# Gather stage: place and counting one-hots compared with numbers in PSUM, bucket numbers as int16, ten short lookups added

## The reference

```python
h1 = relu(einsum('ni,rij->nrj', x, weight1) + bias1)      # 8 relations
h2 = einsum('nrj,rjo->nro', h1, weight2)
msg = h2[src, edge_type] * edge_weight1                   # one row for each edge
agg = segment_sum(msg, dst)                               # layer 1 = relu(agg + bias2)
# layer 2: softmax of edge_weight1 over the edges of one dst, weighted sum of x[src]
# layer 3: two rounds of normalised neighbour sums (dinv[src] * dinv[dst])
# layer 4: gate = silu(attr @ W1.T + b1) @ W2.T + b2 + sum(emb[z[src]] * (emb[z[dst]] @ adaptW.T))
#          msg = gate * x[dst] * (cos cutoff * mult[dst]), summed by src, divided by sum of mult[dst]
```

## Time and profile before

| what | value |
|---|---|
| time, median of 3 runs | 6396.96 us (6395.7 to 6403.15) |
| profiled execution: span, first to last instruction | 5440.4 us |
| what lies around the span | not given by the page; the median is 956.6 us above the span |
| POOL busy | 3976.1 us (73%) |
| DVE busy | 4017.9 us (74%) |
| PE busy, weight loads | 3563.1 us (65%), 2831.5 us (52%) |
| gathers of the stage (L1046) | 1616, 168.0 to 2273.6 us |

### The profile page before, as it was taken

How to read it: one execution, slowest core, us unless ns; L and a number is a source line. 1 busy time by engine, 2 the same in 40 slices (tenths; PEclk the granted TensorE clock), 3 DMA queues, 4 the chain that set the end, 5 groups by cost and what they waited for, 6 DMA issues and landing times.

```text
span 5440.4 us, 122612 instructions
## 1 busy us (share of the span) xinstructions
PE 3563.1 (65%) x46841; PEld 2831.5 (52%) x46841; DVE 4017.9 (74%) x7211; ACT 2632.6 (48%) x5527; POOL 3976.1 (73%) x4023
## 2 busy tenths in 40 slices
PE   8355555555555555347766777777777768988885
PEld 7355555433333333225555555555555568977774
DVE  5555555666666666627888888888888888789999
ACT  2111111111111111226667667677676767888885
POOL 3677777777777777677777777777777764349996
PEclk7555555555555555556666665666676679999998
DMA  5566522222222222124444444444444446877774
GB/s 169 186 211 195 163 60 59 58 68 58 60 59 58 60 59 58 39 40 77 81 75 78 81 76 80 82 80 78 80 79 76 82 90 188 229 200 216 212 213 128
DMA packets 1135509, 576.38 MB, mean 106 GB/s; under 512 B 752611, under 2 KB 1074543, under 8 KB 1134785
## 3 DMA queue, kind: packets, MB, share of 16 engines
q1 hardware_dynamic: 1030017, 457.40, 35.3%
q0 software_dynamic: 104896, 110.96, 9.0%
HBM read 399.84 MB, written 168.16 MB: 104 GB/s over the span
## 4 chain that ended last, share of the span: by engine, by line
POOL 47%; issue 15%; PE 12%; DVE 12%; SPq 6%; DMA 4%; ACT 4%; POOLq 0%; DVEq 0%; ACTq 0%
POOL ring L1046 29%; POOL by_src L1058 9%; PE ps L1612 4%; DMA meta_a<-in_attrT 2%; SPq L866 2%; POOL meta_b L1184 2%; POOL meta_b L1181 2%; PE ps L1436 2%; DVE dst_i L2803 2%; DVE meta_b L2793 2%; DVE big L2824 2%; PE ps L1426 2%; SPq L863 1%; PE ps L1220 1%; POOL ring L1184 1%
## 5 line engine op out<-in xcount | busy, mean ns | idle before, releaser
L1058 POOL DMA_INDIRECT by_src<-meta_a,row_src x1612 | 1624.9, 1008 | 517.1 <-issue 474.3
L1046 POOL DMA_INDIRECT ring<-h_table,meta_b x1616 | 1614.9, 999 | 508.2 <-issue 490.6
L1679 ACT ACTIVATE ring<-ring,meta_b 128x48 f32<-128x48 f32 x1616 | 386.1, 321 | 1727.8 <-DMA ring<-h_table,meta_b 1727.8
L1388 PE MATMUL ps<-ring,WX 128*128 128x48 bf16 x2188 | 417.5, 237 | 894.0 <-DVE row_src L2430 894.0
L1388 PEld LDWEIGHTS ps<-ring,WX 128*128 128x128 bf16 x2188 | 367.0, 168 | 915.1 <-DVE row_src L2430 915.1
L2793 DVE TENSOR_TENSOR meta_b<-big,ps 128x1152 bf16<-128x1152 bf16 (+1 forms) x546 | 698.8, 1280 | 0.0
L1426 PE MATMUL ps<-meta_a,w1T 40*48 40x256 f32 x806 | 381.0, 568 | 465.0 <-DMA meta_a<-in_attrT 282.0
L1518 PE MATMUL ps<-WX,meta_b 128*128 128x49 bf16 (+1 forms) x14742 | 557.3, 197 | 35.7 <-ACT meta_b L1774 16.4
L1518 PEld LDWEIGHTS ps<-WX,meta_b 128*128 128x128 fp8e4 (+1 forms) x14742 | 543.1, 105 | 42.0 <-issue 24.6
L2429 DVE TENSOR_TENSOR row_src<-ring 128x384 f32<-128x384 f32 x202 | 112.7, 558 | 582.6 <-ACT ring L1679 582.4
L1436 PEld LDWEIGHTS ps<-w2T,meta_a 113*128 113x128 f32 x1612 | 325.1, 283 | 338.1 <-issue 297.3
(11 more groups left out here) (388 smaller groups left out, 8954.2 us busy)
## 6 DMA issues: line engine op xcount, KB each, us to landing
by_src<-default SPq DMA_DIRECT2D x44, 1456.0 KB
meta_a<-by_src SPq DMA_DIRECT2D x229, 234.0 KB, 3.9
rb<-lo_rows SPq DMA_DIRECT2D x202, 256.0 KB
rb<-src_rows SPq DMA_DIRECT2D x273, 144.0 KB
rb<-dst_rows SPq DMA_DIRECT2D x273, 144.0 KB
meta_a<-in_attrT SPq DMA_DIRECT2D x402, 80.0 KB
ring<-h_table,meta_b POOLq DMA_INDIRECT x1616
by_src<-meta_a,row_src POOLq DMA_INDIRECT x1612
```

The source lines that it names most:

```text
L1046: pool.indirect_dma_start(ring[:, gg % RING, j, 0:width], None, table, bass.IndirectOffsetOnAxis(ap=index(g * GROUP + j), axis=0)) \
L1058: pool.indirect_dma_start(by_src, bass.IndirectOffsetOnAxis(ap=row_src[:, t:t + 1], axis=0), rec[:, q % RECS, j, :], None).then_inc(s_sc[q ...
L1388: mm = pe.matmul(acc_of(FROM[T] + h, FEAT), hot_w[:, g % 2, h, :, j], rows, start=False, stop=False, skip_group_check=True)
L1679: scaled = act.activation(row, row, ACT.Copy, scale=meta_b[:, t, M_NORM:M_NORM + 1])
```

## The change

Four things are altered.

1. The numbers 0 to 127 lie in PSUM as 32-bit floats (`place_7`, 128 columns of bank 7 behind the 264 columns of the edge terms), and 0 to 49 in bank 6 (`place_6`, written at group 16). The place and counting compares read them there, one number repeated over the tiles of a group by a step of zero. The buffer of repeated bf16 numbers is gone.
2. Since the edge terms share bank 7 with the numbers, `place_hots(g + 1)` runs inside `adapt_group(g)`, between the product and the reduction, and its end now gives the semaphore `s_ejr` on which PE waits before it writes the terms of the next group. The half for the second node block comes first, then the full one. The first group's one-hots are made ahead of the loop.
3. `bucket` is int16. The counting compares are spread over groups 17 to 77 instead of 8 to 77 (`CELL_FROM`).
4. POOL issues ten more lookups in the embedding table behind the sixth, with 128, 127, 126, 124, 120, 112, 96, 80, 64 and 32 rows, into a part of `X` that nobody reads before it is overwritten, and waits for them at the end of the lookups.

```diff
-        bucket = sb("bucket", [P, TILES_IN], BF16)
+        bucket = sb("bucket", [P, TILES_IN], I16)
...
-        place_8 = hot_lo[:, :, :, :].rearrange("p s j n -> p (s j n)").rearrange("p (n j) -> p n j", j=GROUP)
...
-        CELL_FROM = 8
+        CELL_FROM = 17
...
+        place_6 = bank(6, SLOTS)
+        place_7 = bank(7, P, at=GROUP * EJ)
+        PROBES = (128, 127, 126, 124, 120, 112, 96, 80, 64, 32)
+        PROBES_AT = 2 * 3
...
                 gather_embs(embs0, b, embs_in(b)[0])
+                if b + 1 == PROBES_AT:
+                    for i, n in enumerate(PROBES):
+                        pool.indirect_dma_start(probe[0:n, i, :], None, emb_table,
+                                                bass.IndirectOffsetOnAxis(ap=node_z[0:n, b:b + 1], axis=0)).then_inc(s_probe, 16)
+            pool.wait_ge(s_probe, 16 * len(PROBES))
...
                     if g >= 1:
                         pe.wait_ge(s_ejr, g)
+                    else:
+                        pe.wait_ge(s_place, 2)
...
                                              of[:, t:t + n][:, None, :].to_broadcast([P, SLOTS, n]),
-                                             place_8[:, 0:SLOTS, 0:n], ALU.is_equal)
+                                             place_6[:, :, None].to_broadcast([P, SLOTS, n]), ALU.is_equal)
...
-                dve.tensor_tensor(prod_t[:, 0:n, :], terms[:, :, 0:EMB], ring[:, g % RING, 0:n, FEAT:H2W], ALU.mult) \
-                    .then_inc(s_ejr, 1)
+                product = dve.tensor_tensor(prod_t[:, 0:n, :], terms[:, :, 0:EMB], ring[:, g % RING, 0:n, FEAT:H2W], ALU.mult)
+                if hots and g + 1 < GROUPS_IN:
+                    place_hots(g + 1).then_inc(s_ejr, 1)
+                else:
+                    product.then_inc(s_ejr, 1)
...
-                dve.tensor_tensor(hot_w[:, g % 2, 0, :, 0:n], lo_b[:, t:t + n][:, None, :].to_broadcast([P, P, n]),
-                                  place_8[:, :, 0:n], ALU.is_equal)
...
-                                      place_8[:, :, a - t:b - t], ALU.is_equal)
+                                      place_7[:, :, None].to_broadcast([P, P, b - a]), ALU.is_equal)
...
+                return dve.tensor_tensor(hot_w[:, g % 2, 0, :, 0:n], lo_b[:, t:t + n][:, None, :].to_broadcast([P, P, n]),
+                                         place_7[:, :, None].to_broadcast([P, P, n]), ALU.is_equal)
...
-                if g == 0:
-                    place_hots(0)
...
-                if g + 1 < GROUPS_IN:
-                    place_hots(g + 1)
...
+                    if g == CELL_FROM - 1:
+                        link(dve.tensor_copy(place_6, iota[:, 0:SLOTS]))
...
-            dve.tensor_copy(place_8, iota_b[:, 0:P][:, :, None].to_broadcast([P, P, GROUP])).then_inc(s_place, 1)
+            dve.tensor_copy(place_7, iota[:, 0:P]).then_inc(s_place, 1)
```

More of the change, by code:

```diff
@@ L413, in build @@
         s_out = sem("s_out")
+        s_probe = sem("s_probe")
         s_oha, s_abs = sem("s_oha"), sem("s_abs")
@@ L677, in build @@
         place_ps = bank(7, P)
+        place_6 = bank(6, SLOTS)
+        place_7 = bank(7, P, at=GROUP * EJ)
+        assert GROUP * EJ + P <= BANK and CELL_FROM >= MAX_AT + 4
+        PROBES = (128, 127, 126, 124, 120, 112, 96, 80, 64, 32)
+        PROBES_AT = 2 * 3
+        probe = X[:, :, :].rearrange("p b w -> p (b w)")[:, TILES:TILES + len(PROBES) * 2 * EMB] \
+            .rearrange("p (i w) -> p i w", w=2 * EMB)
         gate_at = 6 * QH
@@ L2364, in edge_hots, with adapt_group @@
                 last.then_inc(s_ohe, 1)
-            def adapt_group(g):
+            def adapt_group(g, hots):
                 ts = tiles_of(g)
@@ L2413, in place_hots @@
                                       lo_2[:, g % 2, 0:b - a][:, None, :].to_broadcast([P, P, b - a]),
-                                      place_8[:, :, a - t:b - t], ALU.is_equal)
+                                      place_7[:, :, None].to_broadcast([P, P, b - a]), ALU.is_equal)
                 else:
                     link(dve.memset(lo_2[:, g % 2, 0:1], 0.0))
+                return dve.tensor_tensor(hot_w[:, g % 2, 0, :, 0:n], lo_b[:, t:t + n][:, None, :].to_broadcast([P, P, n]),
+                                         place_7[:, :, None].to_broadcast([P, P, n]), ALU.is_equal)
             def fixed_group(g):
-                n, t = len(tiles_of(g)), g * GROUP
+                n = len(tiles_of(g))
                 rows = ring[:, g % RING, 0:n, 0:FEAT]
                 rest, low = parts_w[:, g % 2, 0, 0:n, :], parts_w[:, g % 2, 1, 0:n, :]
-                if g == 0:
-                    place_hots(0)
                 dve.wait_ge(s_rown, g + 1)
@@ L2430, in fixed_group, with first_layer @@
                 dve.tensor_tensor(low, rest, parts_h[:, g % 2, 0, 0:n, :], ALU.subtract).then_inc(s_w, 2)
-                if g + 1 < GROUPS_IN:
-                    place_hots(g + 1)
-            def first_layer(weights_of):
+            def first_layer(weights_of, hots):
+                if hots:
+                    place_hots(0).then_inc(s_place, 1)
+                else:
+                    dve.memset(red[:, 1, 0:1, 0], 0.0).then_inc(s_place, 1)
                 early = [split(src_i, lo_src, link)]
@@ L2441, in first_layer @@
                         edge_hots(g + 2)
-                    adapt_group(g)
+                    adapt_group(g, hots)
                     if g == 0:
@@ L2473, in _ @@
             with dve.If(dve.value_load(form[0:1, 0:1], min_val=0, max_val=1)):
-                first_layer(edge_group)
+                first_layer(edge_group, False)
             counts, chain[0] = chain[0], counts
             with dve.If(dve.value_load(form[0:1, 1:2], min_val=0, max_val=1)):
-                first_layer(fixed_group)
+                first_layer(fixed_group, True)
             assert chain[0] == counts
```

## The result

The changed kernel takes 6573.07 us (median of 4 runs, 6568.54 to 6580.79), the kernel before in the same job 6396.33 us (6386.64 to 6403.15): ratio 1.0275, 95% interval [1.0261, 1.0290]. It is 177 us slower. Forecast were 6381 us, with 0.11 for slower. The prediction was wrong in its sign, and outside its range.

The account below looks back on a forecast made before the run. POOL issuing gathers was taken as the bound; -16.7 us of stalls and +1.0 us for lookups gave -15.7, so 6396.96 us, including 956.6 us outside the profiled span, became 6381 us, range 6364 to 6396.

Parts of the forecast that it names:

- The 956.6 us carried over: Timed median of 6396.96 us minus profiled span of 5440.4 us, unexplained by any row and added unchanged to the forecast.
- POOL as the bound, 88 us to give back: Gather stage: POOL issues gathers without waiting; 2105.6 us against 2017 undisturbed, so other engines can give back 88 us.
- Stalls removed, 16.7 us: Gathers held by place and counting compares with two SBUF inputs end late; reading PSUM was to save 16.7 us.
- 186 us more on DVE, all hidden: Place and counting compares get longer from PSUM, 186 us in all, all of it beside POOL's gathers.
- If that cover were gone, each microsecond over 10.3 would cost 61 us: Groups 17 to 77: DVE needs 7.4 us per group beside 10.3 us of gathers; any excess costs in 61 groups.
- Order on DVE, and the wait of PE, taken as 0: Moved place and edge compares, PE waiting for place compares: 0 us, with bounds of -5 and +26 us.
- Ten lookups, 1.0 us: Extra lookups ahead of the seventh: POOL's time hidden, their rows load full DMA engines, costing 0 to 1.5, taken 1.0 us.
- Bucket numbers as 16-bit integers: L2292 reading int16 keeps its time: 0 us; at worst it doubles, +0.5 us 49 times.
- DVE becomes the bound: Rival: in groups 17 to 77 counting compares over 0.99 us make DVE the limit; 6426 us, chance 0.03.
- Nothing is given back: Rival: PSUM compares still stop POOL, or as many hits fall on other instructions; 6398 us, chance 0.23.
- The edge compares take over: Rival: moved edge compares L2357 and L2362 delay gathers instead, 26 us more; 6407 us, chance 0.09.
- More is given back: Rival: other late gathers are also freed, 28 us saved in all; 6369 us, chance 0.13.

Follow-up runs that it names:

- e7: The kernel before, unchanged, traced on a chip where it runs slow: 6464.6 us, span 6459.8 us.
- e1: The changed kernel without the ten lookups, on a chip where before takes 5447.16 us: 5425.76 us, ratio 0.9961.
- e4: Before with only the place compares from PSUM, moved behind the product, with PE's new wait: 5441.44 us against 5447.16.
- e8: The full change, run again beside a slow before of 6464.54 us: 6652.15 us, ratio 1.0288.
- e12: Before with place compares still from SBUF, moved behind the product, PE's next edge terms waiting for them: 5471.69 us against 5451.59.
- e11: Before with place compares still from SBUF, moved behind the product, PE waiting for the product alone: 5467.93 us against 5451.59.
- e9: The changed kernel without the ten lookups, beside a slow before of 6464.54 us: 6652.85 us, ratio 1.0282.
- e13: Before with place compares at their old place, made long by 32-bit floats from SBUF: 5516.36 us against 5451.59.
- e5: The full change, run again beside a slow before of 6398.21 us: 6576.68 us, ratio 1.0285.
- e18: The changed kernel without lookups, the product's reduction issued ahead of the place compares: 6463.65 us against a slow before of 6397.89.

## Why the prediction was wrong, by its own steps

- **The 956.6 us carried over.** This is the step that failed: "No row shows what fills that; the page gives no time around the span, and I carry it over unchanged." A trace of the right condition (e7) shows time of this kind inside the program: its span is 1019 us longer than the one I read, 438 of them in the gather stage (2544 in place of 2106 us), the rest in the stages behind it. With that every "hidden beside POOL" lost its ground.
- **POOL as the bound, 88 us to give back.** Right for the trace it was read from, wrong for the timed execution, where POOL waits 452 us for others before the change.
- **Stalls removed, 16.7 us.** Right in mechanism and about in size where it applies: e1 gives 21.4 us back (interval 13.1 to 28.9), with 106 fewer late gathers. The place compares alone give 5.7 of it (e4; 4.2 + 2.0 + 1.6 were reckoned), the other 15.7 come with the counting compares and their new spread (8.9 reckoned), so the sum was closer than its parts. In the long condition the stalls go too (the gathers take 37 us less in e8 than in e7), but an early POOL only waits longer.
- **186 us more on DVE, all hidden.** The size: 1229 ns and 564 ns stand against 1152 and 551 estimated, DVE busy 4239.3 us against 4031.3 in e7, +208. The estimate misread a row: 1276 ns is the median of L2793 over two shapes, not its time at 1152 elements, as the two shapes of the same trace apart show:

```profile
L2793 DVE TENSOR_TENSOR meta_b<-big,ps 128x1152 bf16<-128x1152 bf16 x273 | 367.6, 1347 | 0.0
L2793 DVE TENSOR_TENSOR meta_b<-big,ps 128x1024 bf16<-128x1024 bf16 x273 | 331.2, 1214 | 0.0
```

  With 413 ns at 256 elements and 1347 at 1152 the same working gives 1214 ns at 1024 and 563 at 400, against 1229 and 564 measured. "If that cover were gone, each microsecond over 10.3 would cost 61 us" named the right risk, with the wrong place: what counted was not DVE's load in a group but where in the chain of signals the time was put.
- **Order on DVE, and the wait of PE, taken as 0.** I followed what the moved instructions do to PE and to the gather port, and not who waits behind them: the reduction stands behind the compares, and POOL's ring hangs on it. In the short condition this is covered (e12 against e11: the link +3.8 us, within what can be told); in the long one the position carries 113 of 178 us.
- **Ten lookups, 1.0 us.** Not contradicted, and too small to be told: +3.8 us [-1.6, 9.3] short, 0 long (e8 against e9). Bucket numbers as 16-bit integers were never run alone; the counting compare reading them takes 564 ns, the one reading bf16 563 (e1), and L2292 keeps its time (a median of 566 ns with them in the changed kernel, 567 before).
- **The rivals.** None had the case. "DVE becomes the bound" wanted a compare of over 0.99 us; it took 0.56. "Nothing is given back" is refuted by e1 and e13, and with it what the Trainium skill infers, by which the time would have stayed the same. "The edge compares take over": 50 gathers of 1.016 us in the mean began over the second edge compare (L2362) before, 86 of 1.056 us in e1, some 6 us more (86 x 0.11 - 50 x 0.07); that took back part of the gain and was not decisive. "More is given back" (28 us) can't be told from the forecast: the interval of e1 takes in both.

No version that ran beats before in both conditions. The change without lookups is best in the short one (0.9961), before in the long one; with the reduction first the loss there is 1.1% in place of 2.8%.

## What to carry to other kernels

Check first that the trace and the time belong together: a span of 5440 us beside a median of 6397 us is another execution, and which engine is the bound may differ between the two. When an instruction is moved ahead of another on its engine, list who waits for the ones now behind it, and put first what frees a ring. Work on an engine costs nothing only as long as nobody waits for what stands behind it: the same compares of 1.2 us cost 113 us more ahead of the reduction than behind it (e5, e18), and in the short condition, ahead of it as well, nothing that could be seen (e4).

## What the runs showed of the hardware

- Chips of the same kind ran the unchanged kernel at 5447 to 5452 us and at 6398 to 6471 us. What differs in the traces starts in PE. Up to 3000 us, two weight loads of one line with no semaphore between them start more than 0.45 us apart 829 times in e7 (752 us together) and twice (1.3 us) in the trace ahead of the prediction; the most frequent distance is 0.65 to 0.75 us, the next twice that. It is not the granted clock (0.50 in both between 168 and 2273 us), nor the fetching of instructions by count or duration (383 transfers of 16 KB, 1.08 us in the mean, in both). The trace of e7 also lacks about half of the semaphore events (52641 against 103167), so "remote" here mostly means an event that was not recorded. What makes PE pause is not settled, nor is it shown that its pauses alone make up the whole difference.
- An indirect DMA issued while VectorE runs a compare with both inputs in SBUF took 1.388 us in the mean, 0.947 us over one with one input in PSUM (compares of 1.22 and 1.23 us, e13 and e1).
- A compare with its second input from PSUM cost 1229 ns at 1024 elements and 564 at 400, and one with a repeated input of 32-bit floats from SBUF 1220 at 1024, where two bf16 inputs from SBUF take 685. So the length does not come from PSUM as such. Whether it is the 32-bit floats or the step of zero was not taken apart.
